# Self attention of a decoder layer, rewritten: normalized probabilities in two fp32r parts, projections in thirds between units, and a fixed order of ScalarE's work in each slot

## The reference

```
h  = rmsnorm(layernorm(x)) * norm_w
q, k, v = h @ w_q, h @ w_k, h @ w_v        # 16 heads of 64 columns
ll = q @ k^T / 8, causal, window of 512 rows # here: each sequence is one window
idx = top 128 rows by h @ scorer_w + scorer_b
lg = q @ k[idx]^T / 8, allowed where idx <= own row
o  = softmax over (ll, lg) @ (v, v[idx])
x1 = x + layernorm(x) + o @ w_out
```

## Time and profile before

| what | value |
|---|---|
| median of three runs | 2303.1 us |
| the profiled execution's own time, and its span | 2303.6 us, 2301.9 us |
| self attention in the span | about 0 to 1555 us, eight batches of 188 us |
| busy share over the span: PE, DVE, ACT, POOL | 92%, 57%, 40%, 15% |
| mean granted TensorE clock | 0.945 of full speed |

### The profile page before, as it was taken

One profiled execution on the slowest core, in us unless ns is written; L12 is line 12 of the kernel. 1 busy time (PEld: TensorE's weight loads), 2 busy tenths in 40 slices (PEclk: granted clock), 3 DMA queues, 4 the chain that ended last, 5 costly groups with the idle time before them and its releaser, 6 DMA issues. The chain is left out here.

```text
span 2301.9 us, 36078 instructions
## 1 busy us (share of the span) xinstructions
PE 2120.8 (92%) x12029; PEld 1654.5 (72%) x12029; DVE 1320.5 (57%) x3145; ACT 930.6 (40%) x1989; POOL 343.7 (15%) x605
## 2 busy tenths in 40 slices
PE   3999999999999999999999999996899999978899
PEld 2886787688588688778868868864788888854543
DVE  5584376178167347537717826743787878745401
ACT  3442344244144244334415414424866666413210
POOL 2100100010010010001001001003554445320000
PEclk9999999999999999999999999996987878769899
DMA  5000000100100100000010010002013212150000
GB/s 192 1 2 33 24 1 13 44 1 1 56 1 1 55 3 1 27 31 1 11 47 1 1 57 1 1 33 81 27 59 133 61 58 67 51 201 1 1 0 19
DMA packets 46137, 80.24 MB, mean 35 GB/s; under 512 B 10067, under 2 KB 10067, under 8 KB 45448
## 3 DMA queue, kind: packets, MB, share of 16 engines
q1 hardware_dynamic: 45320, 75.85, 9.9%
q0 software_dynamic: 640, 2.10, 0.2%
HBM read 60.11 MB, written 17.83 MB: 34 GB/s over the span
## 5 line engine op out<-in xcount | busy, mean ns | idle before, releaser
L403 ACT ACTIVATE probs<-s_bank,nmax 128x512 f32<-128x512 f32 (+3 forms) x512 | 249.5, 526 | 368.5 <-DVE nmax L534 266.4
L686 PE MATMUL o_bank<-vals,probs_t 128*128 128x65 f32 x2560 | 329.0, 272 | 0.1
L686 PEld LDWEIGHTS o_bank<-vals,probs_t 128*128 128x128 f32 x2560 | 312.5, 192 | 13.1 <-DVE probs_t L542 12.9
L534 DVE TENSOR_REDUCE nmax<-s_bank 128x1 f32<-128x512 f32 (+2 forms) x384 | 184.4, 508 | 189.2 <-PE s_bank L663 186.5
L710 PE MATMUL pj_bank<-w_o,o_t 128*128 128x512 f32 x512 | 221.8, 594 | 6.0 <-ACT o_t L411 6.0
L542 DVE COPY probs_t<-pt_bank 128x512 f32<-128x512 f32 x320 | 217.8, 681 | 2.2 <-PE pt_bank L671 2.1
L671 PE MATMUL pt_bank<-ident,probs 128*128 128x128 f32 x1280 | 194.9, 275 | 15.7 <-DVE o_t L449 15.7
L659 PE MATMUL s_bank<-k_twice,q_both 128*128 128x512 f32 (+3 forms) x512 | 190.0, 373 | 2.1 <-DVE k_lo L522 2.1
L710 PEld LDWEIGHTS pj_bank<-w_o,o_t 128*128 128x128 f32 x512 | 96.6, 190 | 126.5 <-issue 126.5
L381 ACT ACTIVATE vals<-pj_bank,twice 128x512 f32<-128x512 f32 x64 | 43.9, 688 | 340.4 <-PE pj_bank L583 334.8
L518 DVE SCALAR_TENSOR_TENSOR q_both<-pj_bank,q_both 64x512 fp32r<-64x512 f32 x128 | 88.1, 688 | 141.7 <-ACT q_both L390 139.1
(11 more groups left out here) (268 smaller groups left out, 4125.3 us busy)
## 6 DMA issues: line engine op xcount, KB each, us to landing
xb<-in_x SPq DMA_DIRECT2D x9, 1024.0 KB, 5.8
xt<-x SPq DMA_DIRECT2D x36, 256.0 KB, 2.8
probs<-in_x SPq DMA_DIRECT2D x32, 256.0 KB, 2.6
x<-probs SPq DMA_DIRECT2D x32, 256.0 KB, 2.0
am<-in_L_ffn_attention_mask SPq DMA_DIRECT2D x8, 1024.0 KB, 5.3
out<-x SPq DMA_DIRECT2D x32, 256.0 KB, 2.5
w_sb<-in_L_ffn_w SPq DMA_DIRECT2D x2, 4096.0 KB, 20.4
o_t<-in_L_attn_w_v SPq DMA_DIRECT2D x2, 1024.0 KB, 9.6
```

The source lines that it names most:

```text
L403: ins = nc.scalar.activation(probs[:, i % 2, c0:c0 + nk], s_bank[i % 2][:, c0:c0 + nk], ACT.Exp, bias=nmax[:, i % 4, n:n + 1])
L534: ins = nc.vector.tensor_reduce(nmax[:, i % 4, n:n + 1], s_bank[i % 2][:, c0:c0 + nk], AX.X, ALU.max, negate=True)
L686: ins = nc.tensor.matmul(o_bank[slot][:, o0:o0 + VW], probs_t[:, i % 2, c0 + P * kt:c0 + P * kt + P], vals[:, kt, 2 * p + h, :], start=(kt ...
```

## The change

A unit is now a piece of one head: `unit_rows` gives three units to a head (512 columns; 128 and 384; 256), 48 to a batch. What is done with it, part by part:

- Masks are no matmul any more. Once a batch `tw` turns the chosen rows and VectorE builds `masks` (log 2 for chosen columns, a huge number for later keys).
- `s` on VectorE: one `tensor_tensor_reduce` per block adds the mask to the scores in PSUM, writes the sum to `probs` in SBUF and its row extreme to `nmax`. A score bank comes free after that.
- `s` on ScalarE: the exponential, from `probs` into `probs`, with the row sum into `den`.
- `r`, a new step for unit g-1: VectorE takes the reciprocal of `den`, GpSimd multiplies `probs` with it.
- `t` for unit g-3 turns the normalized probabilities. `turned_hi` for unit g-4: ScalarE copies the high part into `p_hi`. `turned_lo` for the same unit: VectorE subtracts it, giving `p_lo`.
- `pv` once a head: 8 fp32r matmuls, with the values (high and low part side by side as 128 columns) as the stationary operand. The output comes out turned, so `ot` is gone. `o`: ScalarE copies one half of the output bank, VectorE adds the other.
- `q` and `k` projections stand in thirds (4 matmuls) in three successive slots; `q_split` and `k_split` (ScalarE's high part, VectorE's low part) follow in the slot after the last third. The next batch's first pair is projected at the end of a batch, the `ht` steps come earlier (slots 41 to 44).
- The split q and k weights no longer stay in SBUF: before the loop SP stores them to DRAM (`w_pairs`, 8 MB), and in the loop it loads each pair's 1 MB when the buffer's last user is done.

The diff, cut to its core:

```diff
-UNITS = 5
-NU = NPAIR * UNITS
+NH = 2 * NPAIR
+UNITS = 3
+NU = NH * UNITS
+RING = 4
...
+def unit_rows(u):
+
+    return ([(3, 0, 512)], [(0, 0, 128), (2, 128, 384)], [(1, 0, 256)])[u]
...
+    for g in range(-2, NU + 6):
+        if 0 <= g - 1 < NU:
+            plan.append(("r", g - 1))
+        if 0 <= g < NU:
             plan.append(("s", g))
...
+        if 0 <= g - 4 < NU:
+            plan.append(("turned_hi", g - 4))
+        if 0 <= g - 4 < NU:
+            plan.append(("turned_lo", g - 4))
+        if g >= 8 and (g - 8) % UNITS == 0 and (g - 8) // UNITS < NH:
+            plan.append(("o", (g - 8) // UNITS))
+        if g - 1 in thirds and thirds[g - 1][0] in ("q", "k"):
+            plan.append((thirds[g - 1][0] + "_split", thirds[g - 1][1]))
+        if 0 <= g - 3 < NU:
+            plan.append(("t", g - 3))
+        if g >= 7 and (g - 7) % UNITS == 0 and (g - 7) // UNITS < NH:
+            plan.append(("pv", (g - 7) // UNITS))
+        if g in thirds:
+            plan.append(thirds[g])
...
 # GpSimd
+                    if kind == "r":
+                        pl.wait_ge(den_ready, b * NU + i + 1)
+                        for n, (_, c0, nk) in enumerate(unit_rows(i % UNITS)):
+                            part = probs[:, i % RING, c0:c0 + nk]
+                            ins = nc.gpsimd.tensor_tensor(part, part, rden[:, i % 4, n:n + 1].broadcast_to((P, nk)),
+                                                          ALU.mult)
+                        ins.then_inc(norm_ready, 1)
...
 # ScalarE
                     if kind == "s":
                         act.wait_ge(max_ready, b * NU + i + 1)
...
+                        for n, (_, c0, nk) in enumerate(unit_rows(i % UNITS)):
+                            part = probs[:, i % RING, c0:c0 + nk]
+                            ins = nc.scalar.activation(part, part, ACT.Exp, bias=nmax[:, i % 4, n:n + 1], scale=-1.0,
+                                                       accum_out=den[:, i % 4, n:n + 1])
                         ins.then_inc(p_ready, 1)
+                    if kind == "turned_hi":
+                        h, u = divmod(i, UNITS)
+                        slot, ready = pt(b, ("t", i))
+                        act.wait_ge(pt_ready, ready)
+                        if u == 0 and h >= 2:
+                            act.wait_ge(pv_ready, b * NH + h - 1)
+                        n = len(TURN_ORDER[u])
+                        nc.scalar.copy(p_hi[:, h % 2, TURNED_AT[u], :],
+                                       pt_bank[slot][:, 0:P * n].rearrange("p (n k) -> p n k", k=P)).then_inc(hi_ready, 1)
...
 # VectorE
+                    if kind == "q_split":
+                        q_low(b, i)
+                    if kind == "k_split":
+                        k_lows(b, i)
...
+                        nc.vector.memset(carrier[:, 6 + i % 4:7 + i % 4], 0.0)
+                        m0 = MASK_AT[i % UNITS]
+                        for n, (_, c0, nk) in enumerate(unit_rows(i % UNITS)):
+                            ins = nc.vector.tensor_tensor_reduce(
+                                probs[:, i % RING, c0:c0 + nk], s_bank[i % 2][:, c0:c0 + nk],
+                                masks[:, m0 + c0:m0 + c0 + nk], 1.0, 3e38, ALU.add, ALU.min, nmax[:, i % 4, n:n + 1])
                         ins.then_inc(max_ready, 1)
+                    if kind == "r":
+                        dv.wait_ge(p_ready, b * NU + i + 1)
+                        n = len(unit_rows(i % UNITS))
+                        nc.vector.reciprocal(rden[:, i % 4, 0:n], den[:, i % 4, 0:n]).then_inc(den_ready, 1)
+                    if kind == "turned_lo":
+                        h, u = divmod(i, UNITS)
+                        slot, _ = pt(b, ("t", i))
+                        dv.wait_ge(hi_ready, b * NU + i + 1)
...
+                    if kind == "o":
+                        dv.wait_ge(ob_ready, b * NH + i + 1)
...
 # TensorE
                     if kind == "s":
...
                         if i >= 2:
-                            pe.wait_ge(p_ready, b * NU + i - 1)
...
+                            pe.wait_ge(max_ready, b * NU + i - 1)
...
+                        pe.wait_ge(lo_ready, b * NU + UNITS * i + UNITS)
                         if i >= 2:
...
+                            pe.wait_ge(o_ready, b * NH + i - 1)
+                        parts = [(p, k) for p in (p_hi, p_lo) for k in (0, 3, 1, 2)]
+                        for n, (part, k) in enumerate(parts):
+                            ins = nc.tensor.matmul(o_bank[i % 2][:, 0:P * (TT - k)], vals[:, k, i, :],
+                                                   part[:, i % 2, KEYS_AT[k], :], start=(n == 0),
+                                                   stop=(n == len(parts) - 1))
```

More of the change, by code:

```diff
@@ L225, in taken @@
             elif kind == "t":
-                eng.wait_ge(ts_ready, b * NU + i + 1)
-            elif kind == "ot":
-                eng.wait_ge(ot_ready, b * NPAIR + i + 1)
+                eng.wait_ge(lo_ready, b * NU + i + 1)
+            elif kind == "tw":
+                eng.wait_ge(masks_ready, b + 1)
             elif kind == "ht":
@@ L464, in rank, with build_masks @@
                     step(nc.vector.tensor_tensor(cnt[:, 0, :], cnt[:, 0, :], cnt[:, 1, :], ALU.add))
-                    if b is not None:
-                        dv.wait_ge(v_ready, n * (2 * TT))
-                    nc.vector.tensor_scalar(twice[:, :], cnt[:, 0, :], TOPK - 0.5, 1.0, ALU.is_lt,
-                                            ALU.add).then_inc(twice_ready, 1)
+                    nc.vector.tensor_scalar(chosen[:, :], cnt[:, 0, :], TOPK - 0.5, -LN2, ALU.is_lt,
+                                            ALU.mult).then_inc(chosen_ready, 1)
+            def build_masks(b):
+                slot, ready = pt(b, ("tw", 0))
+                dv.wait_ge(pt_ready, ready)
+                row = pt_bank[slot]
+                for at, n in ((0, 3), (640, 2), (1024, 1)):
+                    done.mark(nc.vector.tensor_copy(masks[:, at:at + P * n], row[:, 0:P * n]))
+                for at, k in ((384, 3), (512, 0), (896, 2), (1152, 1)):
+                    ins = nc.vector.tensor_tensor(masks[:, at:at + P], row[:, P * k:P * k + P], later_keys[:, :], ALU.add)
+                done.wait(dv)
+                ins.then_inc(masks_ready, 1)
             def normed(b, n, c):
@@ L497, in _ @@
             split(2)
+            split(3)
+            q_low(None, 0)
+            k_lows(None, 0)
             score_row(None, 0)
-            split(3)
+            split(4)
             for t in range(TT):
                 rank(None, 0, t)
-                if t in (1, 3):
-                    split(4 + t // 2)
-            with dv.Fori(0, B) as b, done.loop(b, 2 * TT + 2 * TT + 1 + NU, B):
+                if t == 1:
+                    split(5)
+            with dv.Fori(0, B) as b, done.loop(b, TT + TT + 2 * TT + 1 + 3, B):
@@ new lines, in _ @@
+                        ins.then_inc(max_ready, 1)
+                    if kind == "r":
[6 more added lines that the diff above has]
+                        dv.wait_ge(hi_ready, b * NU + i + 1)
+                        n = len(TURN_ORDER[u])
+                        nc.vector.tensor_tensor(p_lo[:, h % 2, TURNED_AT[u], :],
+                                                pt_bank[slot][:, 0:P * n].rearrange("p (n k) -> p n k", k=P),
+                                                p_hi[:, h % 2, TURNED_AT[u], :].bitcast(F32),
+                                                ALU.subtract).then_inc(lo_ready, 1)
@@ L560, in _ @@
+                    if kind == "o":
+                        dv.wait_ge(ob_ready, b * NH + i + 1)
+                        rows = head_rows(i % 2)
+                        nc.vector.tensor_tensor(o_t[rows, i // 2, :], o_bank[i % 2][0:HD, :], o_b[rows, :],
+                                                ALU.add).then_inc(o_ready, 1)
                     if kind == "stats":
```

466 lines of the change are left out of this document (254 added, 212 removed).

## The result

The changed kernel takes 3028.2 us (median of 4 runs, 3027.1 to 3031.5) against 2301.9 us before (4 runs, 2300.0 to 2307.0). The ratio is 1.315, with a 95% interval of 1.313 to 1.318. The forecast was 2975 us. The profiled execution took 3031.5 us, with a span of 3029.8.

A forecast was written before the change was run, and what follows sets the result against it. A serial VectorE-ScalarE chain in every slot was taken as the bound. 25 + 170 + 27 + 10 + 29 = 261 us a batch, 269 with clock loss; (269 - 188) x 8 plus 20 gave about 2975 us, range 2770 to 3100.

The forecast's parts named there:

- The chain: In every slot, VectorE's maximum, ScalarE's exponential, `p_hi` and `p_lo` run serially: 170 us a batch; chance 73%.
- The price of `tensor_tensor_reduce`: VectorE's masked maximum costs the same as its addition: 0.69 us at 512 columns, 0.42 at 256.
- The rival of a double price: The new VectorE instruction costs double: 1.9 us more a head, 31 a batch, 3225 us; chance 8%.
- The exponential's row sum, taken at 0: ScalarE's row sum with each exponential lies between 0 and 0.16 us, and was counted as 0.
- The clock, 8 us a batch: TensorE, working in pieces, partly falls to 1.2 GHz: 8 us a batch added, bounds 0 and 25.
- the rival in which the clock makes TensorE a second bound: At 1.2 GHz through all slots a head costs TensorE 11.8 us against 10.6: 3150 us or somewhat more; chance 12%.
- VectorE's other work in the chain, 27 us a batch: Work for the next batch: statistics and scorer products 3 + 3, ranking 6.7, score row 0.7, its turn 2, `ht` slots 12.
- GpSimd hidden: GpSimd's multiplication, 3.1 us a head against 10.6, is wanted two slots later, so costs nothing; otherwise a 512 slot grows 1.2.
- The first slots, tail and output: Per batch: values, projection thirds and first scores 25 us, about 10 after the last exponential, output projection 27.7 and 0.9.
- The start, 20 us: Before the loop, ScalarE's last weight part waits for SP's stores, moving its loop entry from 48.9 to about 69 us.
- TensorE's list, 167 us a batch: TensorE's own work falls from 188 to 167 us a batch, which would be the batch if TensorE stayed the bound.
- The faster rival: TensorE stays the bound, the slots' waits being met early: a batch takes 167 us, 2155 us in all; chance 6%.

The follow-up runs named there:

- square of four kernels: Changed kernel 3028.2 us; with ScalarE's high part ahead of the exponential 2762.7; with other waits moved, exponential still first 2750.8; with both 2528.3.
- clock at 0.92: Changed kernel plus extra TensorE matmuls of constants behind the scores of 512 and 256 units, same order: 2954.0 us, ratio 1.284.
- kernel ordered by need: Changed kernel's instructions on the data, with one written list per engine in the order results are needed: 2234.3 us, 0.973 of the kernel before.
- both edits of order: Changed kernel with high part ahead of exponential, reciprocal behind next maximum, projections a slot earlier, low parts of q and k a slot later: 2528.3 us.

## Why the prediction was right, step by step

- **The chain: right.** The slots of the trace are 2.40 us against 2.5 forecast (512 columns); 3.10 to 3.35 against 3.1 (256); 5.0 to 6.0 against 5.1 (with q); 6.5 to 7.6 against 6.2 (with k and no other work of VectorE, of which up to 1.1 is late scores). The order of ScalarE forces it, as the square of four kernels shows.
- **The price of `tensor_tensor_reduce`: right.** It took 0.68 at 512 columns, as the addition, with a read of 0.08 that the next instruction overlaps. The rival of a double price is out.
- **The exponential's row sum, taken at 0: too low.** Each carries a separate instruction of 0.19 us, and a unit of 128 and 384 columns took 1.01 us to the start of `p_hi` (704.59 to 705.60) where 0.84 was forecast. The 512 unit's 0.84 (701.33 to 702.17) against 0.69 shows the same; there VectorE's back-to-back instructions overlap and give it back.
- **The sum: 8.3 us a batch too low.** The batch came out at 277.3 us (2253.3 - 312.1 over seven batches, by the starts of the output products) against 269, and the forecast was short by 53 us. By amount the gap sits in VectorE's wait for scores, 125.2 us or 15.6 a batch, where 8 were added for a fallen clock. The next three points say what it is made of; only the first two were tried by a run.
- **The clock, 8 us a batch: about right.** With the clock at 0.92 the kernel is 74 us faster, 9.2 a batch, and 77.3 of the 125.2 us of late scores are still there. The rival in which the clock makes TensorE a second bound was thus true to a small part: 74 us, not the 175 it named. Its price was also summed wrongly: 16 heads at 11.8 less 10.6 are 19 us a batch, not 25.
- **VectorE's other work in the chain, 27 us a batch: the mis-sized term.** The score row and the ranking, 9.4 of it, took 13.2 in the slots, as their removal shows. The longest late score, 4.1 us, stands there and is gone with them. Its likely reason is the turn for the score row, priced at 2: it holds up a unit's own turns and with them the next scores. That was not tried by itself, nor was the rest of the 27.
- **GpSimd hidden: not once a batch, a term put at 0.** I had counted its 3.1 us of multiplication a head, and not its 8.0 us of work on the next batch's rows, which stands ahead of it once a batch (666.54 to 674.54). TensorE's turns wait for it there, 4.16 us in the batch shown and 33.2 in all, and VectorE's next maximum is 2.52 us late:

```profile
679.54 0.06 DVE L671 MEMSET carrier<- 128x1 f32 x1 [2.52 <-PE s_bank L822]
```

  Clock 1.2, ranking 3.8 and GpSimd 2.5 add up to 7.5 of the 8.3 us. The GpSimd share is read from one batch, and that the three don't overlap is not shown.
- **The first slots, tail and output: right.** The values and the first unit took 27.8 us to the first reciprocal (644.8 - 617.0), 25 and one slot forecast; the last reciprocal lies 9.7 us ahead of the output projection (857.8 to 867.5), 10 forecast.
- **The start, 20 us: about right.** ScalarE enters the loop at 65.6 us instead of 48.9, 17 us later, and waits there for the store that was named:

```profile
65.63 1.07 ACT L491 CAST vals<-pj_bank 128x512 fp32r<-128x512 f32 x2 [9.78 <-DMA w_pairs<-p_lo]
```

- **TensorE's list, 167 us a batch: about right, and no help.** The kernel ordered by need has 163.5 us of busy TensorE in a batch. The faster rival named the condition: that `p_lo` of a slot can finish before its exponential. The change's order forbids that; the ordered kernel meets it, and comes out 63 us below before, not 148, as its batch is 178 and not 167.

## What to carry to other kernels

When two engines pass work back and forth inside one step of a loop, write down the order of each and ask which instruction of one stands ahead of the result that the other wants: an instruction that could run at once adds to every step when it is queued behind one that waits. Two engines at 40% busy can then bound a kernel (here 44% and 38%), and the saved work of the third comes back as idle time and a lower clock. Test it with a dummy instruction: in the chain a copy of 0.60 us made a slot 0.50 longer, beside it nothing.

## What the runs showed of the hardware

- A row sum on ScalarE is an instruction of its own: 0.19 us (187 ns mean of 506) behind each exponential. In the unit of 128 and 384 columns the next instruction covers 0.10 of it (704.90 + 0.19, next start 705.00); in the 512 unit's slot the high part starts only 0.02 after its end (701.96 + 0.19, 702.17). The exponential itself took 0.72 us at 512 columns, from SBUF with a mask already added; before, from PSUM and without a sum, 0.69.
- Where neighbouring instructions of ScalarE overlap, it is by 0.10 us, so that a copy of 0.60 in the chain cost 0.50 (744.14 to 744.64).
- TensorE's granted clock went with the schedule: 1.00 in the batch before, 0.81 in the batch after, 0.94 in the batch with both edits of order:

```profile
491.80:706.90 215.10, 170.99 (x793) 129.32 (x792) 117.55 (x380) 105.01 (x252) 56.39 (x90) 0.94 0.15 55
```

  The same 793 matmuls took 196.8 us of busy time in the changed kernel and 171.0 here. A better order on the two slower engines thus gave TensorE most of its speed back as well.
